# Last mixture's second products: four places for turned rows, activated rows and results, transposes issued three half tiles ahead

## The chip, the core and the metric

The kernel runs on one core of one Trainium2 chip. A time is the device time of one execution in microseconds (us), and of several executions the median. TensorE (PE) multiplies and transposes and writes to the eight PSUM banks. ScalarE (ACT) applies the activation function and copies, VectorE (DVE) does the rest of the elementwise work. GpSimd (POOL) issues the indirect DMAs (gathers and scatters by a list of row numbers), SyncE (SP) the plain loads and stores. The engines run their own streams of instructions in order and wait for each other by semaphores.

## The reference, cut to what matters

Two transformer layers on 2048 tokens (2 x 1024) of width 256; each has a cross-attention and a mixture. The change lies in the last step, the mixture of layer 1:

```python
# L = 12 weight pairs, hidden width H = 1024, K = 3 of the 12 are chosen per token
h = _apply_mixture(x_flat, dw1, W1)      # sum over the 3 chosen e: dw1[n,e] * (W1[e] @ x[n])
h = jax.nn.gelu(h, approximate=False)
y = _apply_mixture(h, dw2, W2)           # sum over the 3 chosen e: dw2[n,e] * (W2[e] @ h[n])
y = y + dw3 @ b2
```

The first products have 256 inputs and 1024 outputs, the second ones 1024 inputs and 256 outputs. The two mixtures choose their weights apart, so a token goes to three entries of W1 and to three of W2.

## The kernel before

Tokens are sorted by the chosen entry into LT = 59 tiles of 128 places (2048 x 3 places, rounded up for each of the 12 entries). All numbers are float32. The hidden width is cut in two halves of 512, so a tile has two **half tiles**.

**The first products** (`expand`, L2038, 118 of them) write their results to a table in HBM. GpSimd gathers the three results of each token back (`three`, L1964, 48 gathers for each half of the width), VectorE weights and adds them (`combine`, L2241), SyncE stores the sum to the table h_d (`store_sum`, L2308). `SUMS` is 32: 16 token groups times two halves. Those of the second half are still under way when the second products begin.

**The second products** are 118 half tiles in 111 **turns** (`turns_of_products`, L1702). The list of turns has two parts:

- the **first part** is 52 turns of the kind "first" (FIRST = LT - WHOLE = 52), one half tile each, with the first half of the hidden width, which is complete by then;
- the **second part** is 52 turns "second" (the other half of the same tiles) and, mixed among them after every seventh or eighth, 7 turns "whole" (both halves of one tile, two half tiles in one turn). The last turn is a "whole".

The work of one half tile m:

1. `hidden(n)` (L1974) on GpSimd gathers the rows of turn n into one of 7 seats: a "first" into seat i % 7, a "second" into seat i % 5, a "whole" into seats 5 and 6. It first waits until TensorE has transposed what sat there before (semaphore hT_mm, number `u.free`).
2. `turn_hidden(m)` (L2066) on TensorE, four transposes, line L2072, to a bank of psV. I call it **T(m)**.
3. `hidden_T(m)` (L2143) on ScalarE, Gelu from psV to a place of hT (the trace calls it a_W), line L2146: **G(m)**.
4. `contract(m)` (L2076) on TensorE, four products of 128 x 256 (in the trace 8 instructions), line L2089, to a bank of psY: **C(m)**.
5. For a "first" ScalarE copies the result to y_part (`first_part`, L2149; trace: L2150, f_xTk<-f_psY). For the others VectorE adds it to y_part or copies it (L2268, L2265).
6. `scatter(n)` (L1985, line L1988) on GpSimd writes the tile of a "second" or "whole" turn to the table p_d.

psV, hT and psY have two places each, taken in turn by m or by n. psT and psH, the other four banks, are free in this stage. TensorE's order is T(0), then for each m T(m+1), C(m) (L2114 to L2118); ScalarE's is G(m+1), then the copy of m (L2167 to L2173).

GpSimd's order (L2003 to L2021): 4 gathers of hidden rows; then the 48 gathers of `three` with 44 of `hidden` spread among them; then the last 4 of the first part; then a wait until the last sum of VectorE is stored (`all_sums(1)`, L2015), since the second part reads it; then for each turn of the second part a gather and, from the seventh on, the scatter of the turn six before; at the end six scatters more. 

After the last scatter the table p_d is loaded back and added to the output (L2340 to L2345, L2284).

Of the kernel before, what the change touches and what calls it, by code (L numbers as in the profile page):

```python
# [15 lines left out]
P = 128  # L16
# [44 lines left out]
LATE = 4  # L61
TT = B * NT
# [66 lines left out]
def build(nc, t, out):  # L129
# [41 lines left out]
    with ctx:  # L171
# [9 lines left out]
        def attention_weights(stack, a):  # L181


            w = sb(stack, a + "W", [P, 4, KD, D])
            return [w] + [w[:, i] for i in range(4)] + [sb(stack, a + n, shape) for n, shape in (
                ("bk", [P, KD]), ("bq", [P, KD]), ("bvr", [1, D]))]
# [44 lines left out]
        def bias_row(eng, l, done):  # L231
            eng.dma_start(att[l][7][:, :], t[f"a{l}_bv"].rearrange("(a d) -> a d", a=1)).then_inc(done, 16)
# [115 lines left out]
        def value_products(pe, Wv, bvr, place):  # L348
            for b in range(B):
                for k in range(KD):  # L350
                    pe.matmul(place(b), ctxT[:, k, b * S2:(b + 1) * S2], Wv[:, k, :], start=k == 0, stop=False)
                mm = pe.matmul(place(b), ones[0:1, 0:S2], bvr[:, :], start=False, stop=True)
            return mm
# [1162 lines left out]
        def top3_mixture(W, W1, W2, Pw, U, w_ld, w1_ld, w2_ld, load_w1_part, finite):  # L1516
# [9 lines left out]
            with st:  # L1526
# [21 lines left out]
                under = sb(st, "f_under", [P, E1 + 1, E1])  # L1548
                spread = sb(st, "f_spread", [P, E1 + 1, E1])
# [5 lines left out]
                first = sb(st, "f_first", [P, TT])  # L1555
# [10 lines left out]
                pdiv = sb(st, "f_pdiv", [P, TOP, TT])  # L1566
                pmod = sb(st, "f_pmod", [P, TOP, TT])
# [167 lines left out]
                with main:  # L1735
# [11 lines left out]
                    hT = xh.rearrange("p (s k n) -> p s k n", s=2, k=KQ)  # L1747
# [4 lines left out]
                    b2 = sb(main, "f_b2", [P, D])  # L1752
# [6 lines left out]
                    bias_banks = [psT[:, 0, 0:D], psT[:, 1, 0:D], psY[:, 0, 0:D], psY[:, 1, 0:D]]  # L1759
                    sum_banks = [psT[:, 0, :], psT[:, 1, :], psH[:, 0, :], psH[:, 1, :]]  # L1760

# [193 lines left out]
                    with nc.Block() as block:  # L1955
# [68 lines left out]
                        def _(pe):  # L2024
# [41 lines left out]
                            def turn_hidden(m):  # L2066
# [3 lines left out]
                                wait(pe, hT_ready, m - 1)  # L2070
                                for k in range(KQ):
                                    mm = pe.transpose(psV[:, m % 2, k * P:(k + 1) * P],  # L2072
                                                      hg[u.seat + m - u.half][:, k * P:(k + 1) * P], ident[:, :])
                                mm.then_inc(hT_mm, 1)

                            def contract(m):  # L2076
# [6 lines left out]
                                if n < 2:  # L2083
                                    pe.wait_ge(b_done, TT)
                                elif m == u.half:
                                    pe.wait_ge(ya_ready, min(n - 1, FIRST))
                                    wait(pe, yo_ready, n - 1 - FIRST)
                                for k in range(KQ):
                                    mm = pe.matmul(psY[:, n % 2, 0:D], hT[:, m % 2, k, :], W2[c][:, e, k, :],  # L2089
# [24 lines left out]
                            turn_hidden(0)  # L2114
                            for m in range(TILES):
                                if m + 1 < TILES:
                                    turn_hidden(m + 1)
# [12 lines left out]
                        def _(act):  # L2130
# [12 lines left out]
                            def hidden_T(m):  # L2143
                                act.wait_ge(hT_mm, m + 1)
                                wait(act, y_mm, m - 1)
                                act.activation(hT[:, m % 2].rearrange("p k n -> p (k n)"), psV[:, m % 2, :], ACT.Gelu  # L2146
                                               ).then_inc(hT_ready, 1)

                            def first_part(i):  # L2149
                                act.activation(y_part[:, i, :], psY[:, i % 2, 0:D], ACT.Copy).then_inc(ya_ready, 1)  # L2150
# [35 lines left out]
                        def _(dve):  # L2186
# [74 lines left out]
                            for n in range(FIRST, len(turns)):  # L2261
                                u = turns[n]
                                if u.kind == "whole":
                                    dve.wait_ge(y_mm, u.half + 2)
                                    dve.tensor_copy(y_part[:, u.tile, :], psY[:, n % 2, 0:D]).then_inc(yo_ready, 1)  # L2265
                                else:
                                    dve.wait_ge(y_mm, u.half + 1)
                                    dve.tensor_tensor(y_part[:, u.tile, :], psY[:, n % 2, 0:D], y_part[:, u.tile, :], ALU.add  # L2268
# [182 lines left out]
```

## Time and profile before

| | us |
|---|---|
| median of 3 executions | 1159.28 |
| lowest, highest | 1157.64, 1161.54 |
| profiled execution: span from the first to the last instruction | 1216.9 |
| of it, first transpose of the second products (846.9) to the last product's end | 341 |
| of it, after the last scatter's issue (1188.6) to the end | 28 |

The page gives no other time of the profiled execution than its span. The profiled execution is 57.6 us longer than the median of the executions that were only timed. The times in the rows are those of the profiled execution, counted from its first instruction.

### The profile page before, as it was taken

Reading aid. Unit: us, or ns where it says so; the run is one execution under the profiler, and the core shown is the slowest. Engines: PE = TensorE matmul, PEld = TensorE weight load, DVE = VectorE, ACT = ScalarE, POOL = GpSimd, SP = SyncE. Lnnn points to the kernel's source line nnn. Section 1 sums busy time; section 2 is a strip of 40 time slices with the busy share of each in tenths; the row PEclk is TensorE's granted clock in tenths of the full one; section 3 lists DMA queues with packets and bytes.
Section 4 is the critical chain, followed back from the end, with each engine's and each line's share of the span. In section 5 each row is a group of like instructions: output and inputs, shape, how many; then the busy total and the mean of one; then the engine's idle time right before and its main releaser. Section 6 shows DMA issues by size and latency. Waiting matters only on the chain.

```text
span 1216.9 us, 19171 instructions
## 1 busy us (share of the span) xinstructions
PE 1094.3 (90%) x6013; PEld 817.2 (67%) x6013; DVE 552.3 (45%) x1120; ACT 420.3 (35%) x833; POOL 381.8 (31%) x421
## 2 busy tenths in 40 slices
PE   7999899998999999999399999998677888888885
PEld 4888744888998878887244443444566777776773
DVE  4988766764444446776872501333122211111114
ACT  1566544321112225664244432332222232222220
POOL 0221100000220011011154434552666646665650
PEclk8999999998999999999599999998898899999998
DMA  7000130004980029001155578997778865444437
GB/s 208 2 0 0 33 139 1 1 1 161 345 286 9 0 66 382 27 0 47 37 180 200 186 211 295 349 364 276 249 253 278 269 201 179 134 131 142 132 121 281
DMA packets 93410, 187.89 MB, mean 154 GB/s; under 512 B 14109, under 2 KB 34575, under 8 KB 93340
## 3 DMA queue, kind: packets, MB, share of 16 engines
q1 hardware_dynamic: 65346, 109.45, 25.4%
q0 software_dynamic: 23696, 73.69, 19.6%
q10 hardware_dynamic: 4298, 3.81, 1.0%
q8 instruction: 45, 0.74, 0.2%
q14 instruction: 25, 0.20, 0.0%
HBM read 133.56 MB, written 55.44 MB: 155 GB/s over the span
## 4 chain that ended last, share of the span: by engine, by line
PE 40%; issue 4%; DMA 4%; DVE 2%; another core or an unknown queue 2%; ACT 1%; SPq 0%; POOL 0%; POOLq 0%; DVEq 0%; ACTq 0%
PE f_psY L2089 18%; PE f_psH L2046 15%; PE f_psV L2072 4%; DMA W<-in_f_W1T 2%; DMA W<-p_d 2%; PE f_psT L2034 1%; ACT a_W L2146 1%; DVE W L1650 1%; PE f_psV L83 1%; DMA shared<-h_d,f_half_toks 0%; PE f_psH L1929 0%; PE f_psV L1662 0%; SPq L2343 0%; DVE f_xTk L2268 0%
## 5 line engine op out<-in xcount | busy, mean ns | idle before, releaser
L2089 PE MATMUL f_psY<-W,a_W 128*128 x944 | 240.7, 401 | 57.4 <-issue 35.6
L2089 PEld LDWEIGHTS f_psY<-W,a_W 128*128 128x128 f32 x944 | 179.4, 200 | 87.0 <-issue 65.4
L2046 PE MATMUL f_psH<-W,f_xTk 128*128 x472 | 215.5, 596 | 5.7 <-ACT shared L2141 2.0
L2046 PEld LDWEIGHTS f_psH<-W,f_xTk 128*128 128x128 f32 x472 | 84.1, 190 | 96.0 <-issue 95.6
L2146 ACT ACTIVATE a_W<-f_psV 128x512 f32<-128x512 f32 x118 | 70.0, 598 | 155.8 <-PE f_psV L2072 94.8
L2141 ACT ACTIVATE shared<-f_psH 128x512 f32<-128x512 f32 x118 | 70.4, 597 | 142.1 <-PE f_psH L2046 109.5
L1692 POOL DMA_INDIRECT W<-p_d,f_rows x96 | 95.0, 989 | 64.7 <-issue 24.7
L1692 POOL DMA_INDIRECT shared<-h_d,f_half_toks x90 | 87.6, 974 | 85.4 <-DMA p_d<-shared 25.6
L2246 DVE TENSOR_SCALAR a_W<-W,f_wt 128x512 f32<-128x512 f32 x32 | 15.9, 496 | 204.7 <-DMA W<-p_d,f_rows 147.6
L2268 DVE TENSOR_TENSOR f_xTk<-f_psY,f_xTk 128x256 f32<-128x256 f32 x52 | 21.7, 424 | 144.1 <-PE f_psY L2089 112.5
L1692 POOL DMA_INDIRECT a_W<-xn_d,f_toks x59 | 57.6, 975 | 88.9 <-PE f_psT L2034 54.3
L1510 POOL DMA_DIRECT2D m_eos<-m_eo x32 | 16.8, 527 | 202.0 <-DVE m_eo L1407 200.7
L700 POOL TENSOR_TENSOR X<-X,a_bob 128x256 f32 x32 | 24.4, 765 | 162.7 <-DVE a_xn L579 82.6
L1988 POOL DMA_INDIRECT p_d<-f_xTk,f_dest x59 | 58.4, 990 | 45.9 <-DVE f_xTk L2268 25.5
L2072 PE MATMUL f_psV<-ident,shared 128*128 128x128 f32 x360 | 56.5, 282 | 2.3 <-DMA shared<-h_d,f_half_toks 1.7
L1360 PE MATMUL m_psE<-m_eos,m_wu 128*128 128x256 f32 x256 | 57.8, 380 | 0.4 <-DVE m_wu L1436 0.4
L1131 PE MATMUL m_psL<-m_seT,shared 128*128 128x512 f32 x128 | 57.4, 592 | 0.0
L310 POOL TENSOR_TENSOR rstd<-veps,mhalf 128x8 f32<-128x8 f32 (+4 forms) x8 | 13.6, 1696 | 136.7 <-DVE veps L303 136.7
L2072 PEld LDWEIGHTS f_psV<-ident,shared 128*128 128x128 f32 x360 | 46.9, 147 | 13.1 <-DMA shared<-h_d,f_half_toks 2.6
L735 ACT ACTIVATE a_pT<-a_psP 128x256 f32<-128x256 f32 (+2 forms) x96 | 46.8, 490 | 20.2 <-PE a_psP L838 19.0
L2150 ACT ACTIVATE f_xTk<-f_psY 128x256 f32<-128x256 f32 x52 | 20.0, 384 | 93.5 <-PE f_psY L2089 54.0
L1360 PEld LDWEIGHTS m_psE<-m_eos,m_wu 128*128 128x128 f32 x256 | 47.5, 190 | 6.5 <-DVE m_wu L1436 0.7
(299 smaller groups left out, 1867.8 us busy)
## 6 DMA issues: line engine op xcount, KB each, us to landing
p_d<-shared SPq DMA_DIRECT2D x118, 256.0 KB
W<-in_f_W1T SPq DMA_DIRECT2D x24, 512.0 KB, 8.8
W<-in_f_W2T SPq DMA_DIRECT2D x24, 512.0 KB
m_wg<-in_m_Wg SPq DMA_DIRECT2D x16, 512.0 KB, 4.0
m_wu<-in_m_Wu SPq DMA_DIRECT2D x16, 512.0 KB, 5.2
m_wd<-in_m_Wd SPq DMA_DIRECT2D x16, 512.0 KB, 6.1
h_d<-a_W SPq DMA_DIRECT2D x32, 256.0 KB
W<-p_d SPq DMA_DIRECT2D x16, 384.0 KB, 9.2
```

The lines of the kernel that those rows point to most:

```text
L700: pool.tensor_tensor(X[:, s, j], X[:, s, j], bob[:, :], ALU.add).then_inc(xb_ready, 1)
L735: act.activation(pT[:, s, full[0]:full[-1] + 1, :].rearrange("p c n -> p (c n)"), psP[:, g % 2 if g < 2 else 1, 0:len(full) * P], ACT.Copy ...
L1131: mm = pe.matmul(psL[:, n % 2, q * BANK:(q + 1) * BANK], xT[:, n % 2, k, :], seT[:, k, q * BANK:(q + 1) * BANK], start=k == 0, stop=k == K ...
L1360: mm = pe.matmul(psY[:, s, 0:D], ecT[:, s, c, :], eos[:, s, c, :], start=c == 0, stop=c == CS - 1)
L1692: pool.indirect_dma_start(place, None, source, bass.IndirectOffsetOnAxis(ap=index, axis=0)).then_inc(done, 16)
L1988: pool.indirect_dma_start(p2_rows, bass.IndirectOffsetOnAxis(ap=dest[:, i:i + 1], axis=0), y_part[:, i, :], None).then_inc(yo_stored_diag ...
L2046: mm = pe.matmul(psH[:, n % 2, :], xTk[:, i, k, :], W1[c][:, e, k, :], start=k == 0, stop=k == KD - 1)
L2072: mm = pe.transpose(psV[:, m % 2, k * P:(k + 1) * P], hg[u.seat + m - u.half][:, k * P:(k + 1) * P], ident[:, :])
L2089: mm = pe.matmul(psY[:, n % 2, 0:D], hT[:, m % 2, k, :], W2[c][:, e, k, :], start=k == 0 and not (whole and c == 1), stop=k == KQ - 1 and ...
L2141: act.activation(po[:, n % QUAD, :], psH[:, n % 2, :], ACT.Copy).then_inc(po_ready, 1)
L2146: act.activation(hT[:, m % 2].rearrange("p k n -> p (k n)"), psV[:, m % 2, :], ACT.Gelu).then_inc(hT_ready, 1)
L2268: dve.tensor_tensor(y_part[:, u.tile, :], psY[:, n % 2, 0:D], y_part[:, u.tile, :], ALU.add).then_inc(yo_ready, 1)
```

## The change

- `WIDE = 4`: four banks for transposed rows (`hidden_bank(m)`: psV 0, psV 1, psH 0, psH 1), four places for activated rows (`hT`; two of them a new buffer f_hT_more) and four banks for results (`y_banks`: psY 0, psY 1, psT 0, psT 1). All eight banks are in use.
- `LEAD = 3`: TensorE issues T(0), T(1), T(2) first and then T(m+3) ahead of C(m); ScalarE does G(m+3) ahead of the copy of m.
- T(0) to T(3) now wait until ScalarE has emptied the last bank of the first products, and the first four turns, not two, wait for the bias sums.
- To make room, some small tables of the routing (`under`, `spread`, `first`, `pmod`, `pdiv`, `b2`) are put into memory that is free at that time. Their instructions are the same.

GpSimd's program and the seats are unchanged. The diff, cut to its core:

```diff
+WIDE = 4
+LEAD = 3
...
-                    hT = xh.rearrange("p (s k n) -> p s k n", s=2, k=KQ)
+                    hT_more = sb(main, "f_hT_more", [P, 2, HH])
+                    hT = [a.rearrange("p (k n) -> p k n", k=KQ) for a in (
+                        xh[:, 0:HH], xh[:, HH:2 * HH], hT_more[:, 0, :], hT_more[:, 1, :])]
...
+                    wide = [psV[:, 0, :], psV[:, 1, :], psH[:, 0, :], psH[:, 1, :]]
+                    y_banks = [psY[:, 0, 0:D], psY[:, 1, 0:D], psT[:, 0, 0:D], psT[:, 1, 0:D]]
...
                                 pe.wait_ge(hg_ld[u.seat], 16 * u.use)
-                                wait(pe, hT_ready, m - 1)
+                                if m < WIDE:
+                                    pe.wait_ge(po_ready, 2 * LT)
+                                else:
+                                    pe.wait_ge(hT_ready, m - WIDE + 1)
                                 for k in range(KQ):
-                                    mm = pe.transpose(psV[:, m % 2, k * P:(k + 1) * P],
+                                    mm = pe.transpose(hidden_bank(m)[:, k * P:(k + 1) * P],
...
-                                if n < 2:
+                                if n < WIDE:
                                     pe.wait_ge(b_done, TT)
                                 elif m == u.half:
-                                    pe.wait_ge(ya_ready, min(n - 1, FIRST))
-                                    wait(pe, yo_ready, n - 1 - FIRST)
+                                    pe.wait_ge(ya_ready, min(n - WIDE + 1, FIRST))
+                                    wait(pe, yo_ready, n - WIDE + 1 - FIRST)
...
-                            turn_hidden(0)
+                            for m in range(LEAD):
+                                turn_hidden(m)
                             for m in range(TILES):
-                                if m + 1 < TILES:
-                                    turn_hidden(m + 1)
+                                if m + LEAD < TILES:
+                                    turn_hidden(m + LEAD)
                                 contract(m)
...
-                                wait(act, y_mm, m - 1)
-                                act.activation(hT[:, m % 2].rearrange("p k n -> p (k n)"), psV[:, m % 2, :], ACT.Gelu
+                                wait(act, y_mm, m - WIDE + 1)
+                                act.activation(hT[m % WIDE].rearrange("p k n -> p (k n)"), hidden_bank(m), ACT.Gelu
                                                ).then_inc(hT_ready, 1)
...
-                            hidden_T(0)
+                            for m in range(LEAD):
+                                hidden_T(m)
                             for m in range(TILES):
-                                if m + 1 < TILES:
-                                    hidden_T(m + 1)
+                                if m + LEAD < TILES:
+                                    hidden_T(m + LEAD)
```

TensorE, where the second products begin, before: two times four transposes (L2072), then the first product (L2089).

```order
1286 L2072 MATMUL f1_psV<-ident,shared 128x128 x8
1287 L2080 TENSOR_LOAD f_owner
1288 L2080 ISA x2
1289 L2081 ISA
1290 L2089 ISA
1291 L2089 MATMUL f1_psY<-W,a1_W 128x256
```

The same place after the change (L2083 is the transpose, L2100 the product):

```order
1286 L2083 MATMUL f1_psV<-ident,shared 128x128 x8
1287 L2083 MATMUL f1_psH<-ident,shared 128x128 x8
1288 L2091 TENSOR_LOAD f_owner
1289 L2091 ISA x2
1290 L2092 ISA
1291 L2100 ISA
1292 L2100 MATMUL f1_psY<-W,a1_W 128x256
```

Four half tiles are transposed ahead of the first product, not two; in the middle of the stage one T and one C still alternate. TensorE at the end of the stage, before: the last transposes, of the second half of the last "whole", and the product behind them.

```order
2678 L2072 MATMUL f1_psV<-ident,sel 128x128 x4
2679 L2080 TENSOR_LOAD f_owner
2680 L2080 ISA x2
2681 L2081 ISA
2682 L2089 ISA
2683 L2089 MATMUL f1_psY<-W,a1_W 128x256
```

This product is C(116); only C(117) follows. The same place after the change, from the last transposes on; the product in the last row is C(114).

```order
2655 L2083 MATMUL f1_psV<-ident,sel 128x128 x4
2656 L2091 TENSOR_LOAD f_owner
2657 L2091 ISA x2
2658 L2092 ISA
2659 L2100 ISA
2660 L2100 MATMUL f1_psY<-W,f_hT_more 128x256
```

Behind the last transposes, T(117), stand the products of four half tiles, C(114) to C(117), where there were two.

## Rows read from the trace of the kernel before

**Rows 1.** The page: span, and the costliest groups of the stage.

```profile
span 1216.9 us, 19171 instructions
...
L2089 PE MATMUL f_psY<-W,a_W 128*128 x944 | 240.7, 401 | 57.4 <-issue 35.6
...
L1692 POOL DMA_INDIRECT shared<-h_d,f_half_toks x90 | 87.6, 974 | 85.4 <-DMA p_d<-shared 25.6
...
L1988 POOL DMA_INDIRECT p_d<-f_xTk,f_dest x59 | 58.4, 990 | 45.9 <-DVE f_xTk L2268 25.5
```

**Rows 2.** Busy time by stretch: stretch, length, engines (count), granted clock, DMA share, GB/s.

```profile
core 0: us, PE busy (x) PEld busy (x) DVE busy (x) ACT busy (x) POOL busy (x), PEclk, DMA share, GB/s
...
500.00:550.00 50.00, 49.18 (x457) 43.43 (x456) 35.81 (x72) 30.19 (x67) 5.07 (x7) 1.00 0.00 0
...
846.00:1187.00 341.00, 282.10 (x1416) 238.49 (x1416) 56.30 (x107) 93.33 (x194) 210.22 (x215) 0.94 0.58 190
...
756.00:836.00 80.00, 78.31 (x181) 33.86 (x182) 28.15 (x42) 27.34 (x46) 36.57 (x36) 1.00 0.98 350
```

**Rows 3.** Timeline, an even stretch: start, length, engine, line, what, idle before.

```profile
1051.31 0.60 PE L2072 MATMUL f_psV<-ident,sel 128*128 128x128 f32 x4
...
1051.74 1.89 PE L2089 MATMUL f_psY<-W,a_W 128*128 x8
...
1053.18 0.97 POOL L1692 DMA_INDIRECT shared<-h_d,f_half_toks  x1 [0.30 <-issue]
...
1053.67 0.42 DVE L2268 TENSOR_TENSOR f_xTk<-f_psY,f_xTk 128x256 f32<-128x256 f32 x1 [1.74 <-PE f_psY L2089]
...
1054.46 0.99 POOL L1988 DMA_INDIRECT p_d<-f_xTk,f_dest  x1 [0.30 <-issue]
```

**Rows 4.** Timeline, the stretch right behind it, to the next product after a gap.

```profile
1053.91 1.89 PE L2089 MATMUL f_psY<-W,a_W 128*128 x8
...
1055.64 0.60 PE L2072 MATMUL f_psV<-ident,shared 128*128 128x128 f32 x4
...
1056.08 1.89 PE L2089 MATMUL f_psY<-W,a_W 128*128 x8
...
1057.80 0.60 PE L2072 MATMUL f_psV<-ident,shared 128*128 128x128 f32 x4
1059.44 1.08 ACT L2146 ACTIVATE a_W<-f_psV 128x512 f32<-128x512 f32 x2 [4.73 <-PE f_psV L2072]
1059.53 0.42 DVE L2265 COPY f_xTk<-f_psY 128x256 f32<-128x256 f32 x1 [5.43 <-remote]
...
1060.25 1.99 PE L2089 MATMUL f_psY<-W,a_W 128*128 x8 [1.85 <-issue]
```

**Rows 5.** Timeline, GpSimd's first gathers of the stage and TensorE's first transposes.

```profile
843.07 0.94 POOL L1692 DMA_INDIRECT shared<-h_d,f_half_toks  x1 [25.62 <-DMA p_d<-shared]
...
846.86 2.26 PE L2072 MATMUL f_psV<-ident,shared 128*128 128x128 f32 x8 [1.73 <-DMA shared<-h_d,f_half_toks]
...
849.33 0.95 POOL L1692 DMA_INDIRECT shared<-h_d,f_half_toks  x1 [0.31 <-issue]
```

**Rows 6.** Timeline, the seam of the two parts: last sum, then the second part's gathers.

```profile
982.40 0.95 POOL L1692 DMA_INDIRECT W<-p_d,f_rows  x1 [0.30 <-issue]
...
986.30 0.49 DVE L2246 TENSOR_SCALAR a_W<-W,f_wt 128x512 f32<-128x512 f32 x1 [6.94 <-DMA W<-p_d,f_rows]
...
987.62 0.75 DVE L2249 SCALAR_TENSOR_TENSOR a_W<-W,f_wt,a_W 128x512 f32<-128x512 f32 x1
...
1000.70 0.94 POOL L1692 DMA_INDIRECT shared<-h_d,f_half_toks  x1 [10.39 <-PE f_psV L2072]
...
1004.52 0.96 POOL L1692 DMA_INDIRECT shared<-h_d,f_half_toks  x1 [1.22 <-PE f_psV L2072]
...
1005.82 0.60 PE L2072 MATMUL f_psV<-ident,shared 128*128 128x128 f32 x4
```

**Rows 7.** DMA issues of the page: a store's size and time to landing.

```profile
out<-X ACTq DMA_DIRECT2D x16, 128.0 KB, 5.5
```

**Rows 8.** Timeline, the end of the stage: last gather, last transposes, last copy, last scatter.

```profile
1171.49 0.97 POOL L1692 DMA_INDIRECT sel<-h_d,f_toks  x1 [0.30 <-issue]
...
1180.68 0.60 PE L2072 MATMUL f_psV<-ident,sel 128*128 128x128 f32 x4
...
1187.64 0.97 POOL L1988 DMA_INDIRECT p_d<-f_xTk,f_dest  x1 [2.91 <-DVE f_xTk L2265]
```

More of the change, by code:

```diff
@@ L231, in bias_row @@
         def bias_row(eng, l, done):
-            eng.dma_start(att[l][7][:, :], t[f"a{l}_bv"].rearrange("(a d) -> a d", a=1)).then_inc(done, 16)
+            eng.dma_start(att[l][7][0:1, :], t[f"a{l}_bv"].rearrange("(a d) -> a d", a=1)).then_inc(done, 16)
         def half_batch(eng, b, h):
@@ L351, in value_products @@
                     pe.matmul(place(b), ctxT[:, k, b * S2:(b + 1) * S2], Wv[:, k, :], start=k == 0, stop=False)
-                mm = pe.matmul(place(b), ones[0:1, 0:S2], bvr[:, :], start=False, stop=True)
+                mm = pe.matmul(place(b), ones[0:1, 0:S2], bvr[0:1, :], start=False, stop=True)
             return mm
@@ L1547, in top3_mixture @@
                 ones_b = sb(st, "f_ones_b", [P, P], BF16)
-                under = sb(st, "f_under", [P, E1 + 1, E1])
-                spread = sb(st, "f_spread", [P, E1 + 1, E1])
+                under, spread = (carve((E1 + 1) * E1).rearrange("p (a e) -> p a e", e=E1) for _ in range(2))
                 tokid = sb(st, "f_tokid", [P, TT])
@@ L1554, in top3_mixture @@
                 pairi = sb(st, "f_pairi", [P, 2, LT], I32)
-                first = sb(st, "f_first", [P, TT])
+                first = carve(TT)
                 past = sel[:, 0:LT * E1].rearrange("p (i e) -> p i e", e=E1)
@@ L1751, in top3_mixture @@
                     den = sb(main, "f_den", [P, R, TT])
-                    b2 = sb(main, "f_b2", [P, D])
+                    b2 = att[1][7]
                     dwT = shared[:, QUAD * HH:QUAD * HH + TT * EP].rearrange("p (q n) -> p q n", n=P)
@@ L2264, in _ @@
                                     dve.wait_ge(y_mm, u.half + 2)
-                                    dve.tensor_copy(y_part[:, u.tile, :], psY[:, n % 2, 0:D]).then_inc(yo_ready, 1)
+                                    dve.tensor_copy(y_part[:, u.tile, :], y_banks[n % WIDE]).then_inc(yo_ready, 1)
                                 else:
                                     dve.wait_ge(y_mm, u.half + 1)
-                                    dve.tensor_tensor(y_part[:, u.tile, :], psY[:, n % 2, 0:D], y_part[:, u.tile, :], ALU.add
+                                    dve.tensor_tensor(y_part[:, u.tile, :], y_banks[n % WIDE], y_part[:, u.tile, :], ALU.add
                                                       ).then_inc(yo_ready, 1)
```

12 lines of the change are left out of this document (7 added, 5 removed).

## Prediction

> **What bounds the kernel now.** I read the page's groups first, then the busy time by stretch, the timeline of the stage that the change touches, and last the length of the span against the timed executions, which here says most.
>
> The change touches only the second products. In their 341 us TensorE is busy 282 us and idle 59, and ran partly at half clock (0.94 on average) [rows 2]. In other long stretches it hardly idles: 78.3 of 80 us in the first products, 49.2 of 50 in the second attention [rows 2]. So the stage looks as if TensorE had much to win.
>
> The timeline says what the idle time is. In an even stretch T starts at 1051.31, C at 1051.74 and the next C at 1053.91 [rows 3]: T takes 0.43 us, C 1.73, a half tile 2.17 (1055.64 less 1053.91 is 1.73 again [rows 4]). Right behind it something else happens. The product of 1053.91 lasts 1.89 us and is over at 1055.80; the transposes of 1055.64 are over at 1056.24. Their readers, VectorE and ScalarE, start at 1059.53 and 1059.44, together, 3.7 and 3.2 us late, while TensorE goes on with another C and T in between [rows 4]. In the even stretch VectorE starts 0.04 us after the product's end (1051.74 + 1.89 = 53.63, start 53.67 [rows 3]). So TensorE had computed, but its completions reached nobody for 3 to 4 us; then it ran out of activated rows and idled until 1060.25. I call this a **hold**. Such gaps return every 10 to 15 us through the stage, and the 57.4 us of idle time before L2089 [rows 1] are mainly their sum.
>
> Are the holds there when nobody records? The span is 1216.9 us [rows 1] and the median of the timed executions is 1159.28: recording costs 57.6 us. They can hardly lie where TensorE is 98% busy with durations that the clock sets. The stage of the second products has 59 idle us. So I take most of the holds for an effect of recording.
>
> The Trainium skill bears on this in "NOTIFIC — the notification-queue block": its section "7.1 Overflow: three behaviours, one of which stalls the engine" says that the block which writes the profile's records applies backpressure inside rather than lose one, and that this can throttle an engine. Its section "10. Constraints, capacities, measured rates" says the contrary, that a record costs the engine no cycles. By the first the holds vanish in timed runs, by the second they stay; the 57.6 us fit the first. The page gives no time for a hold.
>
> **Without holds GpSimd is the bound.** Its pitch is 0.94 or 0.95 for a gather and 0.30 between two [rows 5], so 1.25 us in the first part; in the second part 0.97 + 0.30 for a gather and 0.99 + 0.30 for a scatter [rows 3], 2.56 us for a turn. The count: 52 gathers of the first part and 48 of `three` make 100 x 1.25 = 125 us; 59 gathers and 59 scatters (the scatters are counted in [rows 1]) make 59 x 2.56 = 151 us. From 843.1 [rows 5] this ends at 1119. TensorE needs 118 x 2.17 = 256 us from 849 (the first C, about 2 us behind its first T at 846.9 [rows 5]), to 1105: less.
>
> One wait of GpSimd must be added, for the last sum. In the trace its last `three` starts at 982.4, VectorE starts 3.9 us later at 986.3 and is done at 987.62 + 0.75 = 988.4 [rows 6]. The store has no landing of its own in the rows; the nearest is a store of 128 KB with 5.5 us [rows 7], which I take. So the sum is there 11.5 us after that `three`. Behind it GpSimd has 1.25 + 4 x 1.25 = 6.3 us of work, so it idles 5.2 us. With 1 us for the last scatter (below) the stage ends at about 1125 without holds. In the trace it ends at 1187.64 + 0.97 = 1188.6 [rows 8], 63.6 later. Of these 57.6 are gone in the timed runs, and 6 are left of which I know nothing. That GpSimd's sum comes so close to the timed median is the main support of this reading. It also caps the gain: GpSimd's program isn't changed, and its idle time in the timed runs is at most 11 us, 5 of them for the sum.
>
> **Part by part.** Small tables moved, the waits of T(0) to T(3) for the last emptied bank, the wait of four turns for the bias: 0. Their work is over before the first gather lands at 846.9 (gather issued at 843.07 [rows 5]).
>
> *Start.* C(0) now comes behind T(3), whose gather is issued fourth, at 843.07 + 3 x 1.25 = 846.8. A gather lands after 846.86 - 843.07 = 3.8 us [rows 5], so T(3) at 850.6 and C(0) at 851.0, 2 us later than before. TensorE has 15 us in hand against GpSimd over the stage. Cost 0, and 2 us if TensorE were the bound.
>
> *Deeper places, same order.* Four banks let TensorE run through a hold of up to 1.1 + 2 x 2.17 = 5.4 us instead of 1.1 (C takes 1.73, Gelu 0.6). In a recorded run this is worth tens of us; in a timed run at most the 6 us left above. I take a third of them, 2 us, because nothing shows what they are.
>
> *The seam.* Let s be the time of the first gather of the second part. GpSimd issues seven gathers and then wants to scatter the first turn: s + 7 x 1.27 = s + 8.9. The gather lands at s + 3.8 [rows 5]; in the trace 1005.82 - 1000.70 = 5.1 is the upper bound [rows 6]. Before, T(52) then runs, C(51), T(53), C(52): 3.8 + 0.43 + 1.73 + 0.43 + 1.89 = 8.3, and VectorE's 0.42 with two hand-overs make s + 8.9. GpSimd doesn't wait. After, TensorE has done C(48) and stands at T(52), because T(m+3) is ahead of C(m). C(49), C(50) and C(51), two of which used to fill this pause, wait behind it. C(52) comes after T(52), C(49), T(53), C(50), T(54), C(51), T(55): 3.8 + 4 x 0.43 + 3 x 1.73 + 1.89 + 0.6 = 13.2. GpSimd waits **4.3 us** more, and being the bound it never makes them up.
>
> *The middle.* A scatter follows the gather of six turns later. After the change C of a turn needs the gather three turns behind it: 3.8 + 0.43 + 1.89 + 0.6 = 6.7 us against three pitches of 2.56 = 7.7. It just holds: 0. If a gather takes 5.1 us, 0.3 us would be lost at a turn.
>
> *The end.* The last gather is issued at h and lands at h + 3.8. Before, C(115), T(117), C(116), C(117) follow T(116); after, C(113), T(117), C(114) to C(117). That is two more products behind the last landing, 2 x 1.73 = **3.5 us**, if TensorE waits for this gather. In the trace it doesn't: the gather is issued at 1171.49 and its rows are turned at 1180.68 [rows 8], since the holds have put TensorE behind; there the term is 0. Before, the last scatter is reached by GpSimd itself at h + 1.27 + 6 x 1.29 = h + 9.0 and by TensorE's way at h + 3.8 + 2 x 0.43 + 2 x 1.73 + 1.89 + 0.6 = h + 10.6, so a wait of 1 to 1.6 us is there already and the 3.5 add in full.
>
> Sum: + 4.3 + 3.5 - 2 = + 5.8 us. Against the profiled execution's own time this sum does not hold, since there the holds are what the deeper places remove; it is made on the 1159.3 us of the timed runs: **1165 us**.
>
> **Rivals.**
>
> *A: the holds, or some, are there in timed runs too, and GpSimd's pitch is shorter without recording.* For it: a hold is seen at TensorE's completions, and nothing in the rows names recording. Against it: the 57.6 us must be somewhere. Then TensorE is the bound at 1105, with 2 us of the start, 5 of the seam: 1112, against 1131 (1188.6 - 57.6) of the timed runs now. The change could win up to 19 us. I price it at half, - 10 us: 1149 us. Another piece speaks for it: in the trace GpSimd's gathers at the seam wait for TensorE's transposes (10.39 us, then 1.22 [rows 6]), and with T two half tiles earlier these waits shrink by up to 4.3 us. The Trainium skill, "Perfetto Trace Analysis", section "Matmul Optimizations", asks for all 8 PSUM banks to be used so that more instructions can overlap; that is this change, and by that rule it is a gain. The rows bear it out for the recorded run only.
>
> *B: nothing to measure.* GpSimd's pitch is a little shorter in timed runs, so that TensorE isn't waiting at the end (0 instead of 3.5) and catches up part of the seam, and small holds give back the rest: 0 to + 3, 1160 us.
>
> *C: the forecast, slower.* It decides as soon as TensorE waits for gathers at the seam and at the end. If gathers take 5.1 us, the middle adds some tenths at some turns; with that and nothing won back it is + 11: 1170 us.
>
> **How the numbers follow.** A measurement of this kernel can tell some 0.3%, 3.5 us, from no change. C has a chance of 0.46, B 0.26, A 0.28. The predicted time is C's, 1165. C's own range is 1163 to 1170. For 8 in 10 the range takes in C, B and the nearer part of A: 1147 to 1170. Faster by over 0.3% is A: 0.28; the same is B: 0.26; slower is C: 0.46.
>
> **What the profile after would show.** Its span is no judge: I expect it shorter than 1216.9, by 10 to 50 us, with less idle time before the products than 57.4 us. Right would be: in even stretches the pitch of 2.17; at the seam a scatter of the first turn that waits for VectorE 4 us or more, with transposes just before it that wait for a gather; at the end four products in a row behind the last transposes. Wrong would be: timed runs that gain what the recorded run gains (then the holds are no effect of recording); GpSimd with long waits in the middle; a pitch of GpSimd other than 1.25 to 1.29.

## The result: 9.3 us slower, and the profile after

| | kernel before | kernel after |
|---|---|---|
| median of 5 executions each, us | 1159.65 | 1168.99 |
| lowest, highest | 1157.64, 1161.98 | 1168.02, 1173.15 |
| ratio, 95% interval | | 1.0087, 1.0068 to 1.0105 |

The profiled execution of the changed kernel took 1170.35 us and its span is 1168.5, so 1.85 us lie outside the span. That is far from the 57.6 us between span and median from which the prediction started. The kernel before was therefore recorded once more (experiment 5). Its span is 1160.4, and this trace, not the one of the rows ahead, is what the changed kernel must be held against. Every execution of this study has a span on record, and its time is 1.8 to 2.0 us longer, on every chip. None is known to have run without recording, so a cost that recording adds to all of them can't be seen here.

The first group of each page that answers to [rows 1], first before (again), then after. With two bank names and two buffers the products of after fall into four groups; this one is the largest, and the idle time before all four is 9.2 us.

```profile
span 1160.4 us, 19171 instructions
...
L2089 PE MATMUL f_psY<-W,a_W 128*128 x944 | 229.7, 387 | 5.9 <-issue 5.0
```

```profile
span 1168.5 us, 19169 instructions
...
L2100 PE MATMUL f_psY<-W,a_W 128*128 x352 | 86.8, 390 | 4.7 <-issue 2.8
```

The idle time before the products is 5.9 and 9.2 us, where [rows 1] has 57.4: the holds of [rows 4] are in neither of these two traces. The granted clock from the first gather of the stage to the last scatter is 0.98 in both, so the clock doesn't explain the difference.

What GpSimd did between its first gather of the second products and its last scatter, its three largest groups (count | busy, mean ns | idle before, and what ended it), before and after:

```profile
L1692 POOL DMA_INDIRECT shared<-h_d,f_half_toks x89 | 86.4, 971 | 33.0 <-issue 22.3 <-PE f_psV L2072 10.8
L1988 POOL DMA_INDIRECT p_d<-f_xTk,f_dest x59 | 58.3, 988 | 22.1 <-issue 14.3 <-DVE f_xTk L2268 4.8 <-DVE f_xTk L2265 2.9
L1692 POOL DMA_INDIRECT W<-p_d,f_rows x48 | 47.3, 985 | 14.6 <-issue 14.6
```

```profile
L1693 POOL DMA_INDIRECT shared<-h_d,f_half_toks x89 | 86.3, 969 | 32.2 <-issue 20.7 <-PE f_psH L2083 5.1 <-DMA h_d<-a_W 4.6
L1996 POOL DMA_INDIRECT p_d<-f_xTk,f_dest x59 | 58.3, 988 | 32.5 <-issue 13.4 <-DVE f_xTk L2281 12.4 <-DVE f_xTk L2278 6.7
L1693 POOL DMA_INDIRECT W<-p_d,f_rows x48 | 46.8, 976 | 14.6 <-issue 14.6
```

GpSimd's busy time is the same. Its gathers of hidden rows don't wait longer (33.0 and 32.2). Its scatters wait 10.4 us longer (22.1 and 32.5), for the results that VectorE makes of TensorE's products. An idle time of 0.30 is only the step from one instruction to the next; what is above it is a wait.

Where in the stage they wait, GpSimd's timeline shows. Four rows of before (again) cut the stage in three: first gather, first scatter, the scatter behind the last gather, last scatter.

```profile
843.57 0.94 POOL L1692 DMA_INDIRECT shared<-h_d,f_half_toks  x1 [26.38 <-DMA p_d<-shared]
...
986.82 1.00 POOL L1988 DMA_INDIRECT p_d<-f_xTk,f_dest  x1 [0.83 <-DVE f_xTk L2268]
...
1120.42 0.99 POOL L1988 DMA_INDIRECT p_d<-f_xTk,f_dest  x1 [0.31 <-issue]
...
1131.69 0.97 POOL L1988 DMA_INDIRECT p_d<-f_xTk,f_dest  x1 [2.91 <-DVE f_xTk L2265]
```

The same of after, with all of the last six scatters:

```profile
841.57 0.94 POOL L1693 DMA_INDIRECT shared<-h_d,f_half_toks  x1 [27.21 <-DMA p_d<-shared]
...
988.75 1.00 POOL L1996 DMA_INDIRECT p_d<-f_xTk,f_dest  x1 [5.33 <-DVE f_xTk L2281]
...
1125.20 0.99 POOL L1996 DMA_INDIRECT p_d<-f_xTk,f_dest  x1 [0.30 <-issue]
1126.56 0.98 POOL L1996 DMA_INDIRECT p_d<-f_xTk,f_dest  x1 [0.38 <-DVE f_xTk L2281]
1128.73 0.97 POOL L1996 DMA_INDIRECT p_d<-f_xTk,f_dest  x1 [1.18 <-DVE f_xTk L2281]
1132.24 0.97 POOL L1996 DMA_INDIRECT p_d<-f_xTk,f_dest  x1 [2.55 <-DVE f_xTk L2281]
1134.41 0.97 POOL L1996 DMA_INDIRECT p_d<-f_xTk,f_dest  x1 [1.20 <-DVE f_xTk L2281]
1136.14 0.98 POOL L1996 DMA_INDIRECT p_d<-f_xTk,f_dest  x1 [0.76 <-DVE f_xTk L2281]
1139.59 0.97 POOL L1996 DMA_INDIRECT p_d<-f_xTk,f_dest  x1 [2.48 <-DVE f_xTk L2278]
```

The differences of these times, and of the same four rows in the traces of the experiments, in us. "To the seam" is from the first gather to the first scatter, "middle" from there to the scatter behind the last gather, "end" from there to the last scatter.

| kernel | to the seam | middle | end | sum |
|---|---|---|---|---|
| before (5) | 143.3 | 133.6 | 11.3 | 288.1 |
| after | 147.2 | 136.5 | 14.4 | 298.0 |
| places only (1) | 143.5 | 133.6 | 11.2 | 288.4 |
| two ahead (2) | 145.0 | 133.6 | 13.1 | 291.7 |
| seam order (3) | 146.4 | 135.9 | 14.7 | 297.1 |
| tail order (4) | 148.4 | 136.9 | 12.0 | 297.3 |
| one ahead until 58 (6) | 143.1 | 135.6 | 14.6 | 293.3 |
| three ahead in the middle only (7) | 142.2 | 135.1 | 12.0 | 289.2 |
| LATE 6 (8) | 144.7 | 133.6 | 11.1 | 289.4 |

After against before: + 3.9 to the seam, + 2.9 in the middle, + 3.1 at the end, + 9.9 in all. One trace of each kernel has an uncertainty of about 1 us in a column (compare 3, 4 and after to the seam, which TensorE reaches by nearly the same way).

### The profile page after: what moved, and what is told of

Read it like the earlier page. It is cut to its first block, busy times and chain, and to the rows that moved or that the text cites. A ratio compares the mean times of both kernels' runs of the same rounds, so it can differ in the third digit from the quotient of the medians.

```text
span 1168.5 us, 19169 instructions
## 1 busy us (share of the span) xinstructions
PE 1082.0 (93%) x6013; PEld 806.1 (69%) x6013; DVE 552.5 (47%) x1120; ACT 424.3 (36%) x833; POOL 380.9 (33%) x421
## 4 chain that ended last, share of the span: by engine, by line
PE 30%; DMA 11%; POOL 4%; issue 3%; DVE 2%; ACT 1%; SPq 0%; DVEq 0%; POOLq 0%; ACTq 0%
PE f_psH L2054 14%; PE f_psY L2100 5%; PE f_psT L2100 5%; DMA shared<-h_d,f_half_toks 3%; DMA p_d<-shared 3%; DMA sel<-h_d,f_toks 2%; DMA W<-p_d 2%; PE f_psV L2083 2%; PE f_psH L2083 2%; POOL W L1693 2%; POOL shared L1693 1%; DMA W<-in_f_W1T 1%; PE f_psT L2042 1%; POOL p_d L1996 1%; DMA sel<-h_d,f_half_toks 1%
## 5 line engine op out<-in xcount | busy, mean ns | idle before, releaser
L2100 PE MATMUL f_psY<-W,a_W 128*128 x352 | 86.8, 390 | 4.7 <-issue 2.8
L2100 PE MATMUL f_psT<-W,f_hT_more 128*128 x336 | 80.6, 383 | 2.8 <-issue 1.8
L2100 PEld LDWEIGHTS f_psY<-W,a_W 128*128 128x128 f32 x352 | 65.0, 195 | 15.0 <-issue 7.7
L1996 POOL DMA_INDIRECT p_d<-f_xTk,f_dest x59 | 58.3, 988 | 32.5 <-issue 13.4
L2100 PEld LDWEIGHTS f_psT<-W,f_hT_more 128*128 128x128 f32 x336 | 60.5, 190 | 11.6 <-issue 4.9
L2158 ACT ACTIVATE a_W<-f_psV 128x512 f32<-128x512 f32 x60 | 35.8, 597 | 65.0 <-PE f_psV L2083 63.9
L1133 PE MATMUL m_psL<-m_seT,shared 128*128 128x512 f32 x128 | 57.4, 593 | 0.0
L2158 ACT ACTIVATE f_hT_more<-f_psH 128x512 f32<-128x512 f32 x58 | 34.6, 597 | 58.4 <-PE f_psH L2083 57.3
L840 PE MATMUL a_psP<-ident,a_pr 128*128 128x128 f32 x320 | 47.4, 278 | 2.7 <-ACT a_pr L729 1.9
```

What stands on the lines that cost most here:

```text
L840: mm = pe.transpose(psP[0:CHR[c], g if g < 2 else 1, (c - cs[0]) * P:(c - cs[0] + 1) * P], pr[:, s, c * P:c * P + CHR[c]], ident[:, :])
L1133: mm = pe.matmul(psL[:, n % 2, q * BANK:(q + 1) * BANK], xT[:, n % 2, k, :], seT[:, k, q * BANK:(q + 1) * BANK], start=k == 0, stop=k == K ...
L1996: pool.indirect_dma_start(p2_rows, bass.IndirectOffsetOnAxis(ap=dest[:, i:i + 1], axis=0), y_part[:, i, :], None).then_inc(yo_stored_diag ...
L2100: mm = pe.matmul(y_banks[n % WIDE], hT[m % WIDE][:, k, :], W2[c][:, e, k, :], start=k == 0 and not (whole and c == 1), stop=k == KQ - 1 an ...
L2158: act.activation(hT[m % WIDE].rearrange("p k n -> p (k n)"), hidden_bank(m), ACT.Gelu).then_inc(hT_ready, 1)
```

## The experiments

The first four ran on one chip, the next four on a second, the last four on a third. On which chip the result above was measured isn't on record. Each is compared with the kernel before on its own chip, five rounds each.

**1. Places only.** The change, with TensorE one half tile ahead as before.

```diff
 WIDE = 4
-LEAD = 3
+LEAD = 1
```

> The changed kernel with LEAD = 1: four places of each kind, the order of before. Order theory (the loss comes from transposes put ahead of products while GpSimd is the bound): as before, 1158 to 1161 us. Places theory (the loss comes from the four banks and places themselves, by sharing or by their waits): as the changed kernel, 1166 to 1171 us. Rival A of the prediction (late completions exist in every run and deeper places hide them): below 1156 us.

Measured: 1159.77 against 1158.76, ratio 1.0006 (0.9991 to 1.0021). The banks, the added places and the moved tables cost and bring nothing that this measurement could tell. The loss is in the order.

**2. Two ahead.**

```diff
-LEAD = 3
+LEAD = 2
```

> The changed kernel with LEAD = 2. Order theory: the cost grows by one product (1.73 us) and one transpose step (0.43 us) at the seam and one product at the end with each step of the lead, so half of the 9.3 us: 1163 to 1165.5 us. A threshold theory (only a lead of 3 exceeds GpSimd's slack in the middle): 1159 to 1161 us.

Measured: 1164.30, ratio 1.0042 (1.0027 to 1.0058), half the loss. By the table the seam costs 1.7, the end 1.8, the middle nothing: about one product of 1.73 us at either place for this one half tile that T runs further ahead.

**3. Seam order.** Three ahead, but from product 50 until seven half tiles into the second part one ahead. In this and the later orders TensorE and ScalarE ask a function how many half tiles are turned before C(m):

```diff
+def turned_by(m):
+    if m < FIRST - 1:
+        return min(m + LEAD + 1, FIRST)
+    return min(m + (2 if m < FIRST + DEEP else LEAD + 1), TILES)
```

> The changed kernel, but at the seam no transpose of the second part is issued before product 50 (a lead of 1 from there on until 7 half tiles into the second part, then 3 again). Order theory: the first scatter no longer waits 5.3 us for its product; 4.3 to 5 us faster than the changed kernel, 1164 to 1165 us. Theory that the loss lies at the end or in the middle alone: 1168 to 1170 us.

Measured: 1168.93, ratio 1.0081 (1.0051 to 1.0110): a miss, nothing was won. TensorE's timeline of this kernel at the seam, with the gathers of GpSimd (T is L2088, C is L2105; the first row is T(51), then C(48) and C(49) in one row, C(50), T(52)):

```profile
976.60 0.60 PE L2088 MATMUL f_psH<-ident,shared 128*128 128x128 f32 x4
977.03 3.62 PE L2105 MATMUL f_psY<-W,a_W 128*128 x16
...
980.49 1.89 PE L2105 MATMUL f_psT<-W,f_hT_more 128*128 x8
982.22 0.60 PE L2088 MATMUL f_psV<-ident,shared 128*128 128x128 f32 x4
982.65 1.89 PE L2105 MATMUL f_psT<-W,f_hT_more 128*128 x8
983.09 0.94 POOL L1693 DMA_INDIRECT shared<-h_d,f_half_toks  x1 [2.16 <-PE f_psV L2088]
...
985.26 0.94 POOL L1693 DMA_INDIRECT shared<-h_d,f_half_toks  x1 [1.22 <-PE f_psV L2088]
...
987.53 1.00 POOL L2001 DMA_INDIRECT p_d<-f_xTk,f_dest  x1 [1.33 <-DVE f_xTk L2286]
```

The first scatter now waits 1.33, not 5.33, but two gathers ahead of it wait for transposes that free their seats (2.16, 1.22). Behind T(51) stand three products without a pause. The same place in the kernel before (again), T(51), C(50), T(52), C(51), T(53), C(52), with GpSimd's first three gathers of the second part:

```profile
976.21 0.94 POOL L1692 DMA_INDIRECT shared<-h_d,f_half_toks  x1 [4.88 <-PE f_psV L2072]
...
977.87 0.94 POOL L1692 DMA_INDIRECT shared<-h_d,f_half_toks  x1 [0.72 <-PE f_psV L2072]
...
979.17 0.60 PE L2072 MATMUL f_psV<-ident,shared 128*128 128x128 f32 x4
...
979.60 1.89 PE L2089 MATMUL f_psY<-W,a_W 128*128 x8
...
980.04 0.95 POOL L1692 DMA_INDIRECT shared<-h_d,f_half_toks  x1 [1.23 <-PE f_psV L2072]
...
981.33 0.60 PE L2072 MATMUL f_psV<-ident,shared 128*128 128x128 f32 x4
...
981.77 1.89 PE L2089 MATMUL f_psY<-W,a_W 128*128 x8
...
983.50 0.60 PE L2072 MATMUL f_psV<-ident,shared 128*128 128x128 f32 x4
...
984.01 1.99 PE L2089 MATMUL f_psY<-W,a_W 128*128 x8
```

Counted from the first gather, T(51) comes at 979.17 - 843.57 = 135.6 before, at 976.60 - 841.11 = 135.5 here, and at 976.60 - 841.57 = 135.0 in after. It is at the same time in all three, though two products fewer have been done ahead of it when T runs three ahead. Those two, 3.46 us, are done behind it, in whatever order: the backlog is made by the last turns of the first part, not by the order at the seam.

**4. Tail order.** Three ahead, shrinking to one over half tiles 100 to 102, and one to the end.

```diff
+def turned_by(m):
+    if m >= TILES - 18:
+        return min(max(m + 2, TILES - 18 + LEAD), TILES)
+    return min(m + LEAD + 1, TILES)
```

> The changed kernel, but the lead shrinks from 3 to 1 over half tiles 100 to 102 and stays 1 to the end. Order theory: two products fewer behind the last landing, 3 to 3.5 us faster than the changed kernel, 1165 to 1166 us. Theory that the loss lies at the seam or in the middle alone: 1168 to 1170 us.

Measured: 1166.74, ratio 1.0054 (1.0038 to 1.0070). The end falls from 14.4 to 12.0, 2.4 us of the 3.1; by the medians the kernel is 2.3 us faster than the changed one, where 3 to 3.5 were expected.

**5. The kernel before, once more.**

> The kernel before, once more. If recording costs what the prediction said, the profiled span is again near 1217 us, some 57 us above the timed executions, with idle time of 50 us and more before the products. If the trace shown of before was one unusual execution, the span is near 1158 us as in the four experiments so far, the pauses of 3 to 4 us are absent, and the rows at the seam show the first scatter of the second part waiting 1 us or less. The ratio should be 1.000 in both cases.

Measured: 1159.16, ratio 0.9995 (0.9983 to 1.0006), span 1160.4 in an execution of 1162.23 us. The rows are above. No holds.

**6. One ahead until half tile 58**, three from there to the end.

```diff
+def turned_by(m):
+    if m < FIRST + DEEP:
+        return m + 2
+    return min(m + LEAD + 1, TILES)
```

> The change, but transposes run one half tile ahead until half tile 58 and three ahead from there to the end. Theory: with three ahead TensorE enters the seam with more products not yet done, and the 4 to 5 us that GpSimd waits there come from that, wherever in the seam the wait shows; so the seam's loss is gone and only the end's is left (2 to 3.5 us): 1161.5 to 1163.5, ratio near 1.003. Rival: the loss is not made in the first part or at its seam but in the second part (scatters behind a whole turn wait 0.8 us each, the end), then nothing is gained: 1168 to 1169, ratio 1.008.

Measured: 1164.82, ratio 1.0035 (1.0022 to 1.0048), against 1.0087 of the change. The way to the seam is back at 143.1. With the miss of 3 this settles it: the seam's loss comes from running three ahead in the first part and shows up at its end.

**7. Three ahead in the middle only**: as 6, and the tail of 4.

> The change with one half tile ahead in the first part, three in the middle of the second (half tiles 59 to about 100), one at the end. By the prediction's middle of 0 it is as the kernel before: 1159 to 1160.5, ratio within 0.1%. If three ahead costs in the middle too (seven whole turns times some 0.8 us of scatter waits), it is 1163 to 1165.

Measured: 1161.97, ratio 1.0013 (1.0002 to 1.0023). Small, but not nothing: the middle costs 135.1 against 133.6. Between 6 and 7 lies the end, 1164.82 - 1161.97 = 2.9 us.

**8. LATE 6** in the kernel before: two more gathers of the first part behind the last gather for the sums.

```diff
-LATE = 4
+LATE = 6
```

> The kernel before with LATE 6, not 4: two more gathers of the first part stand behind the last gather for the sums, so GpSimd waits less for the last sum: 4.4 us less 2 x 1.25 leaves 1.9. If GpSimd is the bound and nothing else is late there, the time falls by up to 2.5 us: 1156.5 to 1157.5, ratio 0.998. If TensorE's transposes, which free the seats, are as late as the sum, the wait only moves to the seats and nothing changes: 1159, ratio 1.000.

Measured: 1163.12, ratio 1.0020 (1.0009 to 1.0030), so neither of the two: slower. The first gather of the second part, GpSimd's timeline:

```profile
977.44 0.94 POOL L1692 DMA_INDIRECT shared<-h_d,f_half_toks  x1 [7.02 <-PE f_psV L2072]
```

It waits 7.02, where the kernel before (again) has 4.88 (976.21 above), and is released by a transpose. The sum may be there earlier, but the seat isn't: with six gathers issued 1.25 us apart TensorE, at 2.17 us for each, is further behind. At the seam of the kernel before the last sum and TensorE are late together: its first gather names a transpose as what released it, and the same gather of the changed kernel, 4.64 us, names the store of the sum. GpSimd is the bound of the stage, but here TensorE stands right beside it.

**The third chip.** The kernel before takes 1221.39 us there (median of 23 executions, 1216.98 to 1225.57; about 1160 on the other chips). The holds are back, as a stretch of experiment 11 shows (its L2072, L2089 and L2268 are those of the kernel before):

```profile
1025.29 1.89 PE L2089 MATMUL f_psY<-W,a_W 128*128 x8
...
1031.48 0.76 DVE L2268 TENSOR_TENSOR f_xTk<-f_psY,f_xTk 128x256 f32<-128x256 f32 x2 [6.00 <-PE f_psY L2089]
1031.54 1.08 ACT L2146 ACTIVATE a_W<-f_psV 128x512 f32<-128x512 f32 x2 [3.06 <-PE f_psV L2072]
1032.18 0.99 POOL L1988 DMA_INDIRECT p_d<-f_xTk,f_dest  x1 [2.18 <-DVE f_xTk L2268]
```

The product ends at 1027.18 and VectorE reads it at 1031.48, 4.3 us later; GpSimd's scatter waits for that. So all that follows is measured in the presence of holds, which the expectations didn't foresee. Their absolute times are for the other chips; what can be held against the measurement are their differences.

**9 and 10. Short products**, in the kernel before and in the changed one:

```diff
-for k in range(KQ):
+for k in (0, KQ - 1):
```

> The kernel before with two of the four products of each half tile left out (the other half of the inputs isn't computed), so TensorE needs 0.43 + 0.87 = 1.3 us for a half tile, not 2.17. GpSimd does all it did. If GpSimd sets the time, only its waits for TensorE go: 0.42 and 0.93 us on seats, 0.53 on the first scatter, 0.97 and 2.61 on the last two scatters, 5.5 us in all; the wait for the last sum stays: 1154 us, ratio 0.995. If TensorE sets it, the stage gets up to 100 us shorter.

> The changed kernel with the same two of four products left out. If the loss is made only by products that stand behind later transposes, it nearly vanishes with short products: at the seam 3.8 + 4 x 0.43 + 3 x 0.87 + 0.95 + 0.6 = 9.7 us against 8.9 that GpSimd has, at the end 8 against 9: within 1 us of the kernel before with short products, 1154 to 1155. If the loss lies in something else of the change (banks, moved tables, ScalarE's order), it stays 9 us above it.

Measured: 1205.34 (1202.48 to 1207.39), ratio 0.9872 (0.9847 to 0.9896), and 1199.97 (1198.87 to 1205.48), ratio 0.9823 (0.9798 to 0.9848). Half of the products' instructions are gone, 118 x 0.87 = 103 us at the pitch of the even stretch, and the time falls by 16 and 21 us. In the stage TensorE is busy only some 67 us less, though: 218.4 us in the trace of experiment 9 (842 to 1174), 285.2 in the one of the rows ahead (842 to 1188), because the granted clock of the stage is 0.78 instead of 0.94. Still the time falls by a quarter of that, so TensorE's amount of work isn't the bound even on this chip. The rest was not as expected: the changed kernel isn't level with the other but 5.4 us ahead by the medians. Where there are holds and the products are short, places and lead may pay; but the granted clock of the stage is 0.84 in experiment 10 against 0.78 in 9, and what of the 5.4 us is the clock's isn't shown. The two intervals just touch, and the changed kernel with its full products was not run on this chip, so whether the change wins or loses there stays open.

**11 and 12. The last whole turn earlier**, with seven and with eight whole turns, in the kernel before:

```diff
-if (i + 1) * WHOLE // FIRST > i * WHOLE // FIRST:
+if i < FIRST - 4 and (i + 1) * WHOLE // (FIRST - 4) > i * WHOLE // (FIRST - 4):
...
-WHOLE = 7
+WHOLE = 8
```

The last two lines are for experiment 12 alone.

> The kernel before, with the seven whole turns spread over the first 48 second turns, not over all 52, so that the last four turns are second ones. The end's wait of GpSimd comes from the last whole: two transposes and three products behind the last landing. With a second turn last it is 3.8 + 0.43 + 1.73 + 1.89 + 0.6 = 8.5 us against the 9.0 that GpSimd needs to reach the last scatter: the waits of 0.97 and 2.61 go, 3 to 3.6 us: 1156.5 us, ratio 0.997. Rival: the wholes, now closer together, make scatters wait in the middle, or the time behind the last scatter grows: 1160, ratio 1.000.

> As the one with the last whole turn earlier, and eight whole turns, not seven: one first and one second less, one whole more, so GpSimd issues one gather less, 1.25 us: 1155 us, ratio 0.996. If the wholes, every sixth turn now, put TensorE behind (each costs it 1.77 us, six turns between them give back 6 x 0.4), no more than the other: 1157.

Measured: 1222.64, ratio 1.0015 (0.9997 to 1.0033), and 1221.73, ratio 1.0000 (0.9983 to 1.0017). Neither wins anything here. From the last gather to the last scatter experiment 11 takes 1193.77 - 1179.84 = 13.9 us, where the trace with holds ahead has 1187.64 - 1171.49 = 16.2 [rows 8]; but experiment 12, whose last four turns are second ones too, takes 1188.04 - 1171.86 = 16.2. So no shorter end is shown: with holds about, one trace of each can't tell. On the chips without holds, for which they were meant, these two versions weren't run. That is open too. No version was found that beats the kernel before.

## Why the prediction was right, and where it wasn't

The sign, the bound and the mechanism came out as predicted: GpSimd sets the time of the stage, its program is unchanged, and products that stand behind later transposes make it wait. The measured + 9.3 us lie above the forecast of + 5.8: the sum had a - 2 for deeper places that isn't there and a 0 for the middle that is + 2.9, and at the seam the amount was right but not the way to it. By its steps:

| step | predicted | measured |
|---|---|---|
| start | 0 | not seen apart |
| deeper places | - 2 | 0 (experiment 1) |
| seam | + 4.3 | + 3.9 (table), gone in experiment 6 |
| middle | 0 | + 2.9 (table), + 1.5 in experiment 7 |
| end | + 3.5 | + 3.1 (table), 2.9 between 6 and 7 |

**The holds.** This is the step whose reasoning was wrong. The prediction put the span of one execution beside the median of others, called the 57.6 us the cost of recording, and called the holds its effect. The traces of before (again), after and experiments 1 to 8 have no holds and the times of the other executions; on the third chip the kernel before takes about 1221 us every time. So the rows ahead most likely come from a chip like the third: their span of 1216.9 and mean granted clock of 0.961 lie within what the 23 executions there have (1215.1 to 1223.6 and 0.954 to 0.964), while the same kernel has 0.970 to 0.979 on the other two. The median beside them comes from one like the first two. The conclusion drawn, to reckon without holds, was right for where the change was measured, by a wrong reason: that was luck, and with a chip like the third for the measurement the forecast would have had no ground. The forecast that the span of after would be 10 to 50 us shorter than 1216.9 came true for the same wrong reason. The passage that the prediction cites from the Trainium skill, "NOTIFIC — the notification-queue block", section 7.1, on backpressure while records are written, isn't borne out: the traces without holds were recorded all the same. Why one chip has them no run here shows.

**Deeper places.** The - 2 was a third of 6 us that came from the same false subtraction. What the sum for GpSimd lacked was no hold: the stage ends at 1132.7 in before (again), not at 1125, with 2.4 us more up to the first gather of the second part, 1.7 more at the seam and 2.6 more at the end. In the traces without holds nothing is there to give back. The rule of the Trainium skill, "Perfetto Trace Analysis", section "Matmul Optimizations", to use all 8 PSUM banks, is experiment 1 in pure form: 1.0006 (0.9991 to 1.0021), no gain where TensorE isn't the bound.

**The seam.** The amount was right (two products and two transposes, 3.46 + 0.87 = 4.3), the place was not. The prediction let TensorE pause at T(52) for the first gather of the second part. TensorE doesn't pause there. In the kernel before T(52) comes 981.33 - 976.21 = 5.1 us behind the issue of its gather, not 3.8, because TensorE is still busy with the four late turns of the first part: T(51), C(50) and T(52) follow each other without a gap. The sign that the prediction named, transposes just ahead of the first scatter that wait for a gather, is missing in the changed kernel too; its T(52) to T(55) wait for none. Therefore seam order (3), which only cured the last link, won no more than the two transposes: C(52) starts 984.82 - 841.11 = 143.7 us after the first gather, in after 986.04 - 841.57 = 144.5, before 984.01 - 843.57 = 140.4. The wait ahead of the second part's first gather was taken as 5.2 and is 4.9 before and 4.6 after. Before, GpSimd was said not to wait at the seam otherwise; it waits 0.42 + 0.93 + 0.53 us (what is above 0.30 in 0.72, 1.23 and 0.83).

**The middle.** Here the prediction put + 0 by a sum that was wrong twice. It took three pitches, 7.7 us, for GpSimd's way from a gather to the scatter that needs it; a gather stands before that scatter, so it is 3 x 2.56 + 1.27 = 9.0, and against the 6.7 us of the product's way a second turn has 2.3 us to spare, not 1.0. And it left out the whole turns. The scatter that waits is that of a whole turn itself, as its releaser shows, the copy L2278. One of them from its gather on, in the timeline of after: gather, its transposes, the transposes ahead of its last product, copy, scatter.

```profile
1081.62 0.97 POOL L1693 DMA_INDIRECT sel<-h_d,f_toks  x1 [0.30 <-PE f_psV L2083]
...
1086.38 0.66 PE L2083 MATMUL f_psH<-ident,sel 128*128 128x128 f32 x4 [0.96 <-DMA sel<-h_d,f_toks]
...
1095.93 0.60 PE L2083 MATMUL f_psH<-ident,shared 128*128 128x128 f32 x4
...
1098.30 0.42 DVE L2278 COPY f_xTk<-f_psT 128x256 f32<-128x256 f32 x1 [3.91 <-PE f_psT L2100]
...
1099.00 0.99 POOL L1996 DMA_INDIRECT p_d<-f_xTk,f_dest  x1 [1.00 <-DVE f_xTk L2278]
```

A whole turn brings two half tiles with one gather. So its last product stands behind the transposes of the fourth half tile after its first, not of the third, and TensorE works through four half tiles of 2.17 us while GpSimd issues three turns of 2.56. The rows come 4.8 us after the issue, the four half tiles take 9.6 (4 x 2.17 = 8.7 and 0.9 lost behind the wait for the rows), product, copy and hand-overs 3.1: 17.4 us. GpSimd would be at the scatter after 6 x 2.56 + 1.27 = 16.7. Five such waits of 0.54 to 1.00 and one of 0.76 behind a second turn make the 2.9 us, less the step of 0.30 in each; the one behind a second turn comes from a gather whose rows were turned 5.6 us after its issue. Before and with two ahead there is no such wait: with T two half tiles ahead the same product is due one half tile, 2.17 us, earlier, which is more than the 0.7 that are lacking. The rows that were read showed T and C of second turns only; the whole turn was known from the code and should have been put through the same sum.

**The end.** As predicted: the last gather is issued at 1123.93, and behind the last transposes the four products run in two blocks of two, up to the copy and the last scatter.

```profile
1128.39 0.66 PE L2083 MATMUL f_psV<-ident,sel 128*128 128x128 f32 x4 [0.41 <-DMA sel<-h_d,f_toks]
...
1131.34 0.60 PE L2083 MATMUL f_psV<-ident,sel 128*128 128x128 f32 x4
...
1131.78 3.62 PE L2100 MATMUL f_psY<-W,f_hT_more 128*128 x16
...
1135.23 3.62 PE L2100 MATMUL f_psT<-W,a_W 128*128 x16
...
1138.89 0.42 DVE L2278 COPY f_xTk<-f_psT 128x256 f32<-128x256 f32 x1 [3.03 <-PE f_psT L2100]
```

The row of 1128.39 shows what the term hung on: these transposes wait for the gather's data. The wait that was there before is 0.97 + 2.61 us, not the 1 to 1.6 of the prediction, since the rows of this gather (both halves of the width) are turned 4.8 us after its issue before and 4.5 after, not 3.8. It is in both kernels and drops out of the difference.

**The rivals.** B (nothing to measure) is ruled out by the interval of the result; it would have needed GpSimd quicker than in the rows, and its gathers take 0.94 to 0.97 in the traces without holds too, some up to 1.27. A (holds in timed executions) is false on two chips and true on the third, where the change itself wasn't run.

## What to carry to other kernels

Issuing an early step further ahead of a late one on an engine that works in order delays the late step by all that is now in front of it. It costs wherever the early step has to wait for data that is not there yet, or where a list ends: at the last turns before a pause of the producer, at items that are longer than the others, and at the tail. If another engine sets the pace and waits for the late step, one step ahead was enough here, and more places alone did no harm. And before a span is set against a median, make sure that both are of the same executions: a difference of 5% was here most likely that between two chips.

## What the runs showed of the hardware that was not expected

The same kernel takes about 1160 us on two chips and 1221 us on a third, in all 23 executions there. In the traces nearly all of the difference lies in the second products: from their first gather to their last scatter it is 288.1 us in before (again), 344.6 in the trace of the rows ahead and 345.5 in that of experiment 11. The first two begin the stage at the same time (843.57 and 843.07), so that all of their difference of 56.5 us lies there; experiment 11 begins it 5 us later. Between 500 and 550 us TensorE is busy 49.19 us in the trace of before (again) and in that of experiment 11. In the 132 us from 842 on they differ. Columns as in [rows 2]; first before (again), then experiment 11:

```profile
500.00:550.00 50.00, 49.19 (x458) 43.45 (x456) 36.17 (x73) 30.20 (x68) 5.06 (x7) 1.00 0.00 0
...
842.00:974.00 132.00, 118.47 (x599) 98.10 (x598) 36.49 (x61) 47.27 (x96) 97.61 (x100) 0.95 0.87 287
```

```profile
500.00:550.00 50.00, 49.19 (x454) 43.42 (x454) 35.12 (x73) 30.33 (x66) 5.08 (x7) 1.00 0.00 0
...
842.00:974.00 132.00, 101.11 (x469) 82.16 (x468) 32.07 (x55) 35.30 (x75) 83.84 (x86) 0.87 0.79 252
```

Experiment 11 begins the stage at 848.28, which is a part of it. GpSimd issues 86 instructions where it issued 100, TensorE is busy 101 us, not 118, and the mean granted clock is 0.87, not 0.95. Indirect DMAs alone don't bring the holds: GpSimd issues 107 of them between 600 and 842 us, and there the trace of the rows ahead loses nothing. Whether the late completions come from TensorE, from the semaphores or from the DMAs isn't shown.
